# Weights split ahead of the layers, the first layer begun before the last batch is normed, and each output block of the last layer written within the loop

## The reference

```python
mod = (silu(c) @ wmod).reshape(B, 6, 1, -1)          # sa, ca, ga, sb, cb, gb; ga and gb clamped
h = layernorm(x) * (1 + ca) + sa
x = x + ga * full_attention(h)                       # one head of 128, over all 1024 tokens
h = layernorm(x) * (1 + cb) + sb
x = x + gb * stack(h)
# stack: 6 layers of
#   x = local_attention(shift(x) @ Wqkv) @ Wo + x    # 16 heads of 64, windows of 32; q, k normed,
#                                                    # scaled by gains and rotated
#   x = (a * gelu(gate)) @ W2 + x                    # a, gate = layernorm(shift(x)) @ W1 + b1
```

## Time and profile before

| what | value |
|---|---|
| median of 3 runs | 3323.32 us (3318.55 to 3324.52) |
| profiled execution | 3324.42 us |
| its span | 3322.6 us, so 1.8 us lie around it |
| busy share of the span | PE 97%, DVE 80%, ACT 74%, POOL 69% |
| matmuls | 62645 |
| mean granted TensorE clock | 0.988 of full |
| DMA | 158 MB, mean 48 GB/s |

### The profile page before, as it was taken

How to read it: one execution, slowest core, us unless ns; L and a number is a source line. 1 busy time by engine, 2 the same in 40 slices (tenths; PEclk the granted TensorE clock), 3 DMA queues, 4 the chain that set the end, 5 groups by cost and what they waited for, 6 DMA issues and landing times. The chain is left out here.

```text
span 3322.6 us, 149878 instructions
## 1 busy us (share of the span) xinstructions
PE 3216.3 (97%) x62645; PEld 2548.6 (77%) x62645; DVE 2647.6 (80%) x6351; ACT 2454.8 (74%) x5069; POOL 2301.0 (69%) x1518
## 2 busy tenths in 40 slices
PE   7979999999999999999999999999999999999997
PEld 5758878777877777887877787777788777778775
DVE  4658878878888887887877888878888887888884
ACT  3437877777777777777777777778777777777774
POOL 2028777777777776777777777777777777777771
PEclk9989999999999999999999999999999999999998
DMA  2001111211211211211121111121111121111111
GB/s 88 3 3 52 46 41 48 70 40 41 56 46 41 74 42 41 55 45 43 49 66 42 48 49 46 41 71 45 48 47 45 43 68 46 50 41 49 46 41 49
DMA packets 98287, 158.06 MB, mean 48 GB/s; under 512 B 18128, under 2 KB 39632, under 8 KB 96720
## 3 DMA queue, kind: packets, MB, share of 16 engines
q1 hardware_dynamic: 93440, 132.73, 14.7%
q10 hardware_dynamic: 4176, 15.74, 1.4%
HBM read 20.48 MB, written 2.10 MB: 7 GB/s over the span
## 5 line engine op out<-in xcount | busy, mean ns | idle before, releaser
L315 POOL TENSOR_TENSOR qks<-work 128x1024 f32<-128x1024 f32 x384 | 911.2, 2373 | 106.4 <-issue 99.3
L323 POOL TENSOR_TENSOR qkr<-qks,rnorm 128x1024 f32<-128x1024 f32 x384 | 732.0, 1906 | 319.3 <-issue 236.1
L492 ACT ACTIVATE sq<-psum 128x512 f32<-128x512 f32 x768 | 460.3, 599 | 307.9 <-PE psum L734 286.8
L331 POOL TENSOR_TENSOR probn<-prob,psumr 128x512 f32<-128x512 f32 x384 | 401.0, 1044 | 310.0 <-DVE psumr L1104 309.9
L734 PE MATMUL psum<-whi,xhi 128*128 128x512 f32 x1152 | 552.2, 479 | 25.9 <-POOL xlo L340 19.2
L1056 DVE TENSOR_REDUCE ssq<-sq 128x8 f32<-128x512 f32 x768 | 518.8, 676 | 8.1 <-ACT sq L492 7.9
L1080 DVE TENSOR_TENSOR work<-psum,rot 128x512 f32<-128x512 f32 x768 | 508.0, 661 | 9.3 <-POOL qks L315 7.2
L757 PEld LDWEIGHTS psum<-kT,qTs 64*32 64x32 f32 x24576 | 362.9, 107 | 155.5 <-issue 128.0
L1098 DVE TENSOR_REDUCE psumr<-prob 128x8 f32<-128x512 f32 x384 | 261.7, 682 | 268.3 <-ACT prob L544 265.2
L734 PE MATMUL psum<-whi,xlo 128*128 128x512 f32 x1152 | 459.4, 399 | 0.0
L734 PE MATMUL psum<-wlo,xhi 128*128 128x512 f32 x1152 | 456.3, 396 | 0.0
(11 more groups left out here) (129 smaller groups left out, 6111.7 us busy)
## 6 DMA issues: line engine op xcount, KB each, us to landing
vsh<-vtok SPq DMA_DIRECT2D x384, 192.0 KB, 2.4
vsh<-vtok SPq DMA_DIRECT2D x384, 64.0 KB, 2.4
xsh<-xs_in SPq DMA_DIRECT2D x192, 64.0 KB, 2.4
ff_x<-x_mid SPq DMA_DIRECT2D x96, 128.0 KB, 2.4
wqkv<-Wqkv_dram ACTq DMA_DIRECT2D x5, 1536.0 KB, 7.4
wo_next<-Wo_dram ACTq DMA_DIRECT2D x5, 512.0 KB, 10.1
...
```

The costliest lines, as they stand in the source:

```text
L315: pool.tensor_tensor(qks[:, :, :], rcos, rsin, ALU.add).then_inc(s["add_ready"], 1)
L323: pool.tensor_tensor(qkr[:, n % 2, :, :], qks[:, :, :], rnorm[:, :].unsqueeze(2).to_broadcast([P, 2 * OCT, DH]), ALU.mult).then_inc(s["qkr ...
L331: pool.tensor_tensor(probn[:, :, :], prob[:, n % 2, :, :], psumr[:, n % 2, 1, :].unsqueeze(2).to_broadcast([P, OCT, KEYS]), ALU.mult).then ...
L492: act.activation(sq[:, w * OCT:(w + 1) * OCT, :], bank[w].rearrange("p (h n) -> p h n", n=DH), ACT.Square).then_inc(s[("sqq_ready", "sqk_r ...
```

## The change

**1. Weights and rotary tables are made in the head.** POOL multiplies the rotary table by the gains of all six layers (6 instructions of 2048 columns) and splits all Wqkv in 18 pieces of 1024 columns (a copy and a subtraction each), between the norms. Layer 0 stays in SBUF; for layers 1 to 5 SP stores the results in DRAM (5 tables of 1 MB, 15 pieces of 1 MB) and fetches them back at the border of each layer: six sections and two halves of the table of 512 KB each, each as soon as its last reader in the old layer is done. The buffers of this stage lie where `kT`, `vtok` and others lie later, so POOL clears these only when all stores have landed, and PE waits for that (`overlays_set`) with its first projection. ACT's and POOL's work at the border is gone, and so is `rotary_gains` for each tile. `wo` is fetched straight into place in step 6 of the new layer, on SP's queue.

**2. The layers begin earlier.** The second norm of the last batch has its own buffer, and is made at step 1 (DVE) and step 2 (PE, ACT) of the layers. The norm of the next batch is placed one tile earlier in the head.

**3. The output within the loop.** Each block of the last layer is scaled and transposed at place 6 of its turn and added and stored at place 7, with bank 4 and buffers of its own (`yT`, `yout`).

The core of the diff:

```diff
+SECTION_AT = {wo: k for k, wo in enumerate(SECTIONS)}
+PIECES = len(SECTIONS) // 2
...
+        xn_last = sb("xn_last", [P, TPB, D])
...
+            rot_raw = early.enter_context(nc.sbuf_tensor("rot_raw", [P, TPB, 2 * 2 * DH], F32))
+            qk_gain = early.enter_context(nc.sbuf_tensor("qk_gain", [P, DEPTH, 2 * 2 * DH], F32))
+            wraw = early.enter_context(nc.sbuf_tensor("wraw", [P, 2, 2, 512], F32))
+            rstage = shared("rstage", [P, 2, TPB, 2 * 2 * DH])
+            wstage = early.enter_context(nc.sbuf_tensor("wstage", [P, 2, 2, 2, 512], F32R))
...
+        vtok = sb("vtok", [P, 2, UPT, OCT * DH])
...
+        kT = sb("kT", [P, HEADS // 2, WIN + 2 * P])
...
+        wsplit = nc.dram_tensor("wsplit", (DEPTH - 1, len(SECTIONS), P, 2 * 512), F32, kind="Internal").ap()
+        rsplit = nc.dram_tensor("rsplit", (DEPTH - 1, P, TPB * 2 * 2 * DH), F32, kind="Internal").ap()
...
+            def raw_fetched(j):
+                layer, k = j // PIECES, j % PIECES
+                sp.dma_start(wraw[:, j % 2, :, :].rearrange("p s n -> p (s n)"), Wqkv[layer][:, k * 1024:(k + 1) * 1024]).then_inc(wraw_in[j % 2], 16)
+
+            def split_stored(j):
+                layer, k = j // PIECES, j % PIECES
+                sp.dma_start(wsplit[layer - 1, 2 * k:2 * k + 2].rearrange("s p n -> p s n"),
+                             wstage[:, j % 2, :, :, :].bitcast(F32).rearrange("p s h n -> p s (h n)")).then_inc(w_stored[j % 2], 16)
+
+            raw_fetched(0)
+            raw_fetched(1)
...
+            for layer in range(1, DEPTH):
+                sp.wait_ge(s["rot_made"], layer + 1)
+                sp.dma_start(rsplit[layer - 1], rstage[:, layer % 2, :, :].rearrange("p t n -> p (t n)")).then_inc(r_stored[layer % 2], 16)
+            for j in range(DEPTH * PIECES):
+                sp.wait_ge(s["w_lo"], j + 1)
+                if j + 2 < DEPTH * PIECES:
+                    raw_fetched(j + 2)
+                if j >= PIECES:
+                    split_stored(j)
...
+            def section_renewed(layer, k):
...
+                w, oc = SECTIONS[k]
+                if layer == 1 and k == 0:
+                    for half in range(2):
+                        sp.wait_ge(w_stored[half], 16 * ((DEPTH * PIECES - PIECES + half) // 2))
+                sp.wait_ge(s[("projq_ready", "projk_ready", "vp_ready")[w]], layer * UNITS - 1 + oc)
+                sp.dma_start(wparts[:, k, :, :].bitcast(F32).rearrange("p h n -> p (h n)"), wsplit[layer - 1, k]).then_inc(wparts_in[k], 16)
...
+            def rotation_renewed(layer, half):
...
+                sp.wait_ge(s["rotk_ready"], layer * UNITS - (1 - half) * UNROLL)
+                sp.dma_start(rot[:, half * TPI:(half + 1) * TPI, :, :, :].rearrange("p t k n d -> p (t k n d)"),
...
+            def output_renewed(layer):
...
+                sp.wait_ge(s["wo_ready"], layer * TILES)
+                sp.dma_start(wo[:, :, :].rearrange("p k n -> p (k n)"), Wo[layer]).then_inc(s["wo_in"], 16)
...
+                    sp.wait_ge(s["gout_ready"], 2 * (B - 1))
+                if n == UNITS - UNITS // B:
                     sp.wait_ge(s["gout_ready"], 2 * B)
...
+            def stored(k):
...
+                sp.wait_ge(s["yo_ready"], k + 1)
+                sp.dma_start(out_v[k], yout[:, :, :]).then_inc(s["y_sent"], 16)
...
+                section_renewed(renewed_at(step, 0), SECTION_AT[1, 1])
...
+                stored(last_block_at(step, 7))
+                rotation_renewed(renewed_at(step, -6), 0)
+                section_renewed(renewed_at(step, -2), SECTION_AT[0, 0])
+                section_renewed(renewed_at(step, -2), SECTION_AT[1, 0])
+                section_renewed(renewed_at(step, -1), SECTION_AT[0, 1])
+                section_renewed(renewed_at(step, 1), SECTION_AT[2, 0])
+                section_renewed(renewed_at(step, 2), SECTION_AT[2, 1])
+                rotation_renewed(renewed_at(step, 2), 1)
+                output_renewed(renewed_at(step, 6))
...
+            def rotary_gains(layer):
+                if layer >= 3:
+                    pool.wait_ge(r_stored[layer % 2], 16 * ((layer - 1) // 2))
+                dst = rstage[:, layer % 2, :, :] if layer else rot[:, :, :, :, :].rearrange("p t k n d -> p t (k n d)")
+                pool.tensor_tensor(dst, rot_raw[:, :, :], qk_gain[:, layer:layer + 1, :].to_broadcast([P, TPB, 4 * DH]),
+                                   ALU.mult).then_inc(s["rot_made"], 1)
+
+            def weights_split(j):
+                layer, k, slot = j // PIECES, j % PIECES, j % 2
+                pool.wait_ge(wraw_in[slot], 16 * (j // 2 + 1))
+                if j in (PIECES, PIECES + 1):
+                    pool.wait_ge(r_stored[1], 16 * 3)
+                    pool.wait_ge(r_stored[0], 16 * 2)
+                elif layer:
+                    pool.wait_ge(w_stored[slot], 16 * ((j - PIECES) // 2))
+                parts = wstage[:, slot, :, :, :] if layer else wparts[:, 2 * k:2 * k + 2, :, :]
+                pool.tensor_copy(parts[:, :, 0, :], wraw[:, slot, :, :]).then_inc(s["w_hi"], 1)
+                pool.wait_ge(s["w_hi"], j + 1)
+                pool.tensor_tensor(parts[:, :, 1, :], wraw[:, slot, :, :], parts[:, :, 0, :].bitcast(F32), ALU.subtract).then_inc(s["w_lo"], 1)
 
             global_inverse(0)
-            for k in range(len(SECTIONS)):
-                weights_low(0, k)
-            for n in range(1, 2 * B):
-                global_inverse(n)
+            pool.wait_ge(s["gain_in"], 16 * 2)
+            pool.wait_ge(s["gvs_ready"], 2)
+            for layer in range(4):
+                rotary_gains(layer)
+            global_inverse(1)
+            pool.wait_ge(s["gxn_ready"], 2)
+            for layer in range(4, DEPTH):
+                rotary_gains(layer)
+            done = 0
+            for n, pieces in ((1, 2), (2, 3), (3, 3), (4, 3), (5, 3), (6, 4)):
+                if n > 1:
+                    global_inverse(n)
+                    pool.wait_ge(s["gxn_ready"], n + 1)
+                for j in range(done, done + pieces):
+                    weights_split(j)
+                done += pieces
+            for half in range(2):
+                pool.wait_ge(w_stored[half], 16 * ((DEPTH * PIECES - PIECES + half) // 2))
+            pool.memset(kT[:, :, 0:WIN], 0.0)
+            pool.memset(vtok[:, 1, :, :], 0.0).then_inc(s["overlays_set"], 1)
...
+            x_low(0)
+            global_inverse(2 * B - 1)
...
-                low_renewed(renewed_at(step, -1), 0, 1)
-                low_renewed(renewed_at(step, 0), 2, 3)
-                low_renewed(renewed_at(step, 2), 4)
-                low_renewed(renewed_at(step, 3), 5)
-                rotary_gains(step)
-                x_low(step)
+                if step:
+                    x_low(step)
                 probabilities(step - 5)
...
-            def weights_high(layer, k):
...
-                act.wait_ge(s["wo_in"], layer * 16 + 16)
-                act.wait_ge(s["wo_ready"], layer * TILES)
-                act.activation(wo[:, :, :], wo_next[:, :, :], ACT.Copy).then_inc(s["wo_moved"], 1)
...
-                weights_fetched(renewed_at(step, -8))
-                output_renewed(renewed_at(step, 6))
-                high_renewed(renewed_at(step, -1), 0, 1)
-                high_renewed(renewed_at(step, 0), 2, 3)
-                high_renewed(renewed_at(step, 2), 4)
-                high_renewed(renewed_at(step, 3), 5)
...
+                if step == 2:
+                    for half in range(2):
+                        normed_second(B - 1, half)
...
+                if n == 0 and w == 0:
+                    pe.wait_ge(s["overlays_set"], 1)
...
+                if n == 0:
+                    pe.wait_ge(s["gout_ready"], 2 * B)
...
-                    pe.wait_ge(s["wo_moved"] if tile else s["wo_in"], tile // TILES if tile else 16)
+                    pe.wait_ge(s["wo_in"], tile // TILES * 16 + 16)
...
+            def turned_back(k, step):
+                if k is None:
+                    return
+                pe.wait_ge(s["y_ready"], k + 1)
+                need(pe, "pts_ready", min(step - 4, STEPS))
+                for i in range(TPI):
+                    mm = pe.transpose(bank[4][:, i * P:(i + 1) * P], yT[:, i * P:(i + 1) * P], ident[:, :])
+                mm.then_inc(s["y_tr"], 1)
...
+                                   (last_block_at(step, 7), "yo_ready", lambda k: k + 1))
...
+                turned_back(last_block_at(step, 6), step)
...
-            for i in range(BLOCKS // 2):
-                for h in range(2):
-                    n = i * 2 + h
-                    pe.wait_ge(s["y_ready"], n + 1)
-                    if h == 0:
-                        need(pe, "yo_ready", n)
-                    for k in range(4):
-                        mm = pe.transpose(bank[h][:, k * P:(k + 1) * P], yT[:, h, k * P:(k + 1) * P], ident[:, :])
-                    mm.then_inc(s["y_tr"], 1)
+                if step == 2:
```

(43 more changed lines are left out.)

157 lines of the change are left out of this document (63 added, 94 removed).

## The result

The changed kernel takes 3271.19 us (median of 4 runs, 3269.35 to 3272.99) beside 3321.44 us for the kernel before on the same chip: a ratio of 0.9849, with a 95% interval of 0.9831 to 0.9866. In a later series it was 3270.04 beside 3323.74 (0.9837, 0.9824 to 0.9850). I had predicted 3271.

The account below looks back on a forecast made before the run. PE, busy 97% of the span, was taken as the bound, with gains only in its gaps. From 3324.4 us, -37.2 - 3 - 5.3 - 7.7 = -53.2 gave 3271.2, predicted as 3271; range 3257 to 3299.

Parts of the forecast that it names:

- Borders, the size: Turns at five layer borders: 28.5 us excess across them and 8.7 us behind them removed, 37.2 us together.
- Borders, the reason: Layer borders: PE's 2.63 us wait for `xlo` put down to POOL's two low parts, 2.51 us, directly ahead.
- The clock's dip goes with the gap: Behind the border gap: a matmul takes 0.80 us, later ones 0.50; the clock dip was taken to go with the gap.
- The turn ahead of a border: Turn before each border: 5.8 us excess in all while weights transfer; 3 us gain taken, bounds 5.8 either way.
- The slower rival: Layers and head: every bulk transfer stops PE, at 1.2 us each giving 3359 us; chance 0.04.
- Head: Before and into the layers: first projection 8.6 us earlier at 219.7, other terms +3.5, -2.2, +2; sum -5.3 us.
- the rival of stores at half rate: Head: 1 MB stores go at half the rate, PE starts at 230.5, 13 us more, 3284 us; chance 0.14.
- The norm in the layers: Steps 1 and 2, as the pipeline fills: the moved norm costs between 2.1 and 5.7 us, 3.5 taken.
- The three rotary rows off POOL: Head: three tables of 0.73 us no longer stand on POOL, the chain there; 2.2 us gained.
- The norm of batch 3: Head: it stands on POOL behind three pieces, DVE waits 4.6 us; 0 to 4.6 reaches PE, 2 taken.
- Tail: End and last layer: 12.4 us gained, last fetch 1.7 us later, loop transposes 3.0 us; sum -7.7 us.
- The rival of the lock: Last layer and step 1: DVE's scaling waits for a 2.37 us POOL row in six blocks, 3287 us; chance 0.08.

Follow-up runs that it names:

- border_pool: The changed kernel with six spare subtractions of 512 columns on POOL at each of the five borders: 3271.85 us, ratio 0.9852 to the kernel before.
- border_rows: The changed kernel with six spare ACT copies, six spare POOL subtractions and one POOL product at each border, no waits between them: 3274.96 us, one run.
- border_chain: As border_rows, with ACT's copies waiting for the old layer's last projections and POOL's subtractions for those copies: 3299.73 us, one run.
- fetch_twice: The changed kernel with each of the six weight sections at a border fetched a second time into an unread buffer: 3318.81 us, ratio 0.9993.
- wo_wait: The changed kernel with ACT waiting in step 6 of each new layer for the output matmuls, then copying 1024 columns: 3279.73 us, ratio 0.9863.
- section 3: The bulk-transfer experiment, run as fetch_twice (3318.81 us); its stops are PE standing with no wait shown, each after a late 16 KB instruction transfer.
- norm_first: The changed kernel with the last batch's second norm put ahead of the layers again: 3275.62 us, ratio 0.9852 to the kernel before.

## Why the prediction was right, and where it was not

- **The sum.** Right in its main terms, and lucky in its last digit. The lines of the table miss by up to 2.7 us each, in both directions, and add up to 0.6; the 0.2 us between 3271 and the median is chance. Against the median beside it the gain is 50.3 us, where I had said 52.
- **The bound.** Right. Ordinary turns take 62.51 us in all kernels here, and every microsecond gained was a gap of PE, or the clock behind one.
- **Borders, the size.** Right: 26.7 of the 28.5 us, and 7.0 of 8.7 for `wo`. What is left is `x_half` behind a section (up to 1.3 us at one border), one stop of 0.84 us and a few small gaps.
- **Borders, the reason.** Half wrong. "The wait for `xlo` comes from POOL" named the row directly ahead. That row alone brings back under 1 us a border (border_pool), all rows together 1.6 (border_rows); with POOL's wait for ACT and rows as long as those of before it is 6.4 (border_chain). So the step that failed is the cause of the wait: it was a queue without slack behind a wait for ACT, 1.65 us, and not POOL's rows alone. I took the 28.5 us as a whole from the turn marks, not from the rows, and so the sum came out right in spite of it.
- **The clock's dip goes with the gap.** Right, and shown from both sides: 1.00 behind a gap of 0.81 us (border_rows), 0.53 and 0.50 behind 2.93 and 6.29 us (border_chain, fetch_twice). What a gap between these costs the runs show at single places only: 1.62 us left the clock at 1.00 (wo_wait), 2.09 us did not (fetch_twice).
- **The turn ahead of a border.** Mis-sized: I took 3 of 5.8 us, and 5.7 went. The four stops of the kernel before, 0.85 to 1.50 us, are of the kind of section 3, and one of 0.84 us is left in the changed kernel, behind the last border. That the large transfers made them is likely by the timing shown there, but no run tests it. The slower rival, that each bulk transfer stops PE, fell with fetch_twice: 30 transfers more, and three stops.
- **Head.** The chain of pieces and stores came within 2 us at each step, and the rival of stores at half rate fell: a store of 1 MB lands in 6.4 us by the page, where I had 7.5. The norm in the layers cost 4 us with the clock's share (predicted 3.5). The three rotary rows off POOL gave nothing that shows where I took 2.2: norm_first has none of them and needs 111.7 us to the first mark, the kernel before 111.4, though at a clock of 0.94 and not 0.97. The norm of batch 3 behind three pieces makes DVE wait 5.1 us and PE 3.99 us for `sq` in the changed kernel, but PE had waited 3.16 there before, and by 171.8 us both kernels stand at the same matmul: 0 where I took 2. So in the head too two terms that were off cancel, -2.2 and +2.
- **The head's scatter** I had not reckoned with. Ten profiles of kernels with the same head have the first turn mark from 330.95 to 335.40 us, 333.0 in the mean. The one of the result was the latest of them, so -4.4 in the table is the least; by the mean it is -6.7, beside one profile of the kernel before. Most of it arises ahead of the layers: attention ends at 212.5 to 215.5 us in these ten. Why is open.
- **Tail.** -9.0 us by the profiles where I had -7.7. The loop pays 0.44 us in each of five turns and 1.2 in the sixth, 3.3 in all (predicted 3.0), the fetch is 1.55 us late (predicted 1.7), and behind it 13.9 us are gone (predicted 12.4), so the end comes 12.3 us earlier (predicted 10.7). The scaling never waits for POOL: its eight rows last 437 to 486 ns. The rival of the lock fell here, since POOL waits for the reciprocal ahead of it and starts its row 0.16 us behind the scaling's, but what the rule says does happen, in the head, where I had not looked for it.
